# The self-attention readout of a decoder layer: sixteen 128x64 products in place of thirty-two 128x32 ones

## The chip, the cores and the metric

The kernel runs on one core of a Trainium2 chip. The metric is the device time of one execution in microseconds (us). Before the change three runs gave 231.12, 231.74 and 231.94 us, with a median of 231.74.

## The reference, cut to what matters

One pre-norm decoder layer on x of shape (32, 64, 256): self-attention with 16 heads of 16 (causal), an attention over a context of 64 rows per sequence (single head, masked), and a feed-forward block whose activations and weights are quantised.

```python
def _L0_attn_ref(x, W_qkv, W_out):
    qkv = jnp.einsum('bsd,ed->bse', x, W_qkv)
    ...
    scores = jnp.einsum('bhqd,bhkd->bhqk', Q, K) / jnp.sqrt(jnp.float32(D_K))
    scores = jnp.where(causal_mask, jnp.float32(-jnp.inf), scores)
    attn = jax.nn.softmax(scores, axis=-1)
    out = jnp.einsum('bhqk,bhkd->bhqd', attn, V)      # the readout
    ...
    return jnp.einsum('bsd,ed->bse', out, W_out)

x = x + _L0_attn_ref(_layernorm(x), W_qkv, W_out)
x = x + _L0_xattn_ref(_layernorm(x), ctx_2048, mask_BxS2_bk0)
x = x + _L0_ffn_ref(_layernorm(x), gate_w, down_w, gate_norm_w, down_norm_w)
```

## The kernel before, in words

The 2,048 rows of x are cut into T = 16 tiles of 128 rows, two sequences of 64 in each. All engines work through the same stages of every tile, each engine in an order written out by hand, and semaphores in `ev` say when a stage of tile t is done. Several tiles are under way at a time: on TensorE the attention of tile s runs beside the feed-forward of tiles s - 3 to s - 5.

TensorE's order stands in three parts. Lines 509 to 573 are a prologue, written out call by call, with the readouts of tiles 0 to 3. Then `step` (line 575) is the order of one tile's time, and a loop on TensorE's own registers (line 596) runs five turns of two steps, with the readouts of tiles 4 to 13. Lines 602 to 654 are the end, written out, with the readouts of tiles 14 and 15. In a step the order is readout, transpose_ya, cross_readout, gate_up_1, gate_up_0, transpose_yx, transpose_readout, project_qk, cross_scores, the transposes of h, project_out, scores_k, down, transpose_cross_weights, project_v, scores_q, transpose_z.

The readout multiplies the unnormalised weights `pT` by the values `v2`. ScalarE writes `pT` (line 716) from the transposed scores: on its 128 partitions lie the 64 keys of two heads of a pair, and along it the 128 queries of the tile (64 of sequence 0, then 64 of sequence 1), once for each of 8 pairs. `v2` (lines 110 and 705) is block-diagonal: for each sequence b and pair i it holds 2 x 17 columns, the 16 values and a column of ones for each head, zero on the other head's partitions. So a product has a contraction of 128, streams 34 columns of `v2`, and has some columns of `pT` as its stationary operand. It writes to PSUM bank 2, `o_ps[rows, i, :, :]`, with the queries on the partitions.

Before the change four products of 32 queries each serve one pair i (line 414): query block k goes to partitions 32k to 32k + 31, that is, to a tile of the array of 128 rows by 32 columns, and takes the values of sequence k // 2. That makes 8 x 4 = 32 products for one tile of x. All operands are float32, for which a product shows as two weight loads and two matmuls in the trace, so a readout is 64 loads and 64 matmuls there.

The readout waits for `v_d` (ScalarE has written `v2`), `exp_d0` and `exp_d1` (the halves of `pT`), and the events that free bank 2. After it come VectorE's reciprocal of the sums (line 1204) and the scaling into `oN` (line 1209), TensorE's transpose of `oN` and the output projection. `freed` (line 301) issues the waits for the former users of a bank; `within` (line 287) wraps one in a branch when its tile number is a loop variable, and returns a null context for a plain number.

Of the kernel before, what the change touches and what calls it, by code (L numbers as in the profile page):

```python
# [14 lines left out]
SEQ = 64  # L15
# [41 lines left out]
def decoder_kernel(nc, x, ctx_n, ctx_t, mask, wqkv_t, wout_t, gate_t, down_t, g_gate, g_down, const, bits, out):  # L57
    T = x.shape[0]
    with ExitStack() as stack:
        def sb(name, shape, dt=F32):  # L60
            return stack.enter_context(nc.sbuf_tensor(name, shape, dt))
# [48 lines left out]
        v2 = sb("v2", [P, 2, 2, PAIRS, 2, VW])  # L110
# [4 lines left out]
        pT = sb("pT", [P, 2, PAIRS, P])  # L115
# [34 lines left out]
        def bank(k, columns):  # L150
            return ps[:, k, 0:columns]
# [8 lines left out]
        o_ps = bank(2, PAIRS * 2 * VW).rearrange("p (i j d) -> p i j d", i=PAIRS, j=2)  # L160
# [110 lines left out]
        def _(pe):  # L271
            kept = {}

            def at(t):

                if isinstance(t, int):
                    return t
                if t.base not in kept:

                    kept[t.base] = pe.snap(t.turn * 2 + t.base if t.base >= 0 else (t.turn * 2 + t.base) & 31)  # L280
                    pe.compute_val(kept[t.base])
                return kept[t.base]
# [4 lines left out]
            def within(t, least, most):  # L287

                if isinstance(t, int):
                    return nullcontext()  # L290
                low, high = (least - t.base + 1) // 2, (most - t.base) // 2
                if low > 0 and high < TURNS - 1:
                    return pe.If((t.turn >= low) & (t.turn <= high))
                if low > 0:
                    return pe.If(t.turn >= low)
                return pe.If(t.turn <= high) if high < TURNS - 1 else nullcontext()
# [4 lines left out]
            def freed(users):  # L301

                for name, count in users:
                    with within(count, 1, T):
                        pe.wait_ge(ev[name], at(count))

            def transposes(dst, src, chunks, done, identity=ident):
# [11 lines left out]
            def transpose_ya(t, *users):  # L319
                pe.wait_ge(ev["ya_d"], at(t + 1))  # L320
                freed(users)
                transposes(xT_ps, ya[:, t % 2, :], DC, ev["yaT_ps"])

            def project_qk(t, *users):
                pe.wait_ge(ev["yaT_d"], at(t + 1))
                freed(users)
                if first(t):
                    pe.wait_ge(wqk_in, 16)
                for e in range(2 * DC):
                    for c in range(DC):  # L330
                        last = pe.matmul(qk_ps[:, e * P:(e + 1) * P], wqk[:, c, e * P:(e + 1) * P], yaT[:, t % 2, c, :],  # L331
                                         start=(c == 0), stop=(c == DC - 1))
                last.then_inc(ev["qk_ps"], 1)

            def project_v(t, *users):
                pe.wait_ge(ev["yaT_d"], at(t + 1))
                freed(users)
                if first(t):
                    pe.wait_ge(wv_in, 16)
                for b in range(2):  # L340
                    for c in range(DC):
                        for j in range(2):
                            last = pe.matmul(v_ps[SEQ * j:SEQ * (j + 1), b * P:(b + 1) * P], yaT[:, t % 2, c, b * SEQ:(b + 1) * SEQ],  # L343
                                             wv[:, c, j * P:(j + 1) * P], start=(c == 0), stop=(c == DC - 1))
                last.then_inc(ev["v_ps"], 1)
# [59 lines left out]
            def readout(t, *users):  # L405
                pe.wait_ge(ev["v_d"], at(t + 1))
                freed(users)
                for half in range(2):
                    pe.wait_ge(ev[f"exp_d{half}"], at(t + 1))
                    for g in (2 * half, 2 * half + 1):  # L410
                        for c in range(DC):
                            i = 4 * c + g
                            for k in range(4):
                                last = pe.matmul(o_ps[32 * k:32 * (k + 1), i, :, :], pT[:, t % 2, 2 * g + c, 32 * k:32 * (k + 1)],
                                                 v2[:, t % 2, k // 2, i, :, :], start=True, stop=True)
                last.then_inc(ev["o_ps_d"], 1)

            def transpose_readout(t, *users):
# [101 lines left out]
            scores_k(0, ("mx_d", 1), ("mT_d", 1))  # L520
            transpose_ya(2, ("yaT_d", 2))
            readout(0, ("q_d", 2), ("k0_d", 2), ("k1_d", 2))
            scores_q(1, ("exp_d0", 1), ("exp_d1", 1))
            project_qk(2, ("oN_d", 1))
# [3 lines left out]
            scores_k(1, ("mx_d", 2), ("mT_d", 2))  # L528
            project_out(0)
            readout(1, ("q_d", 3), ("k0_d", 3), ("k1_d", 3))  # L530
            weight_totals(("x1_d", 1))
            transpose_ya(3, ("oT_d", 1))
# [7 lines left out]
            cross_scores(0, ("yxT_d", 1))  # L540
            scores_q(3, ("exp_d0", 3), ("exp_d1", 3))
            readout(2, ("q_d", 4), ("k0_d", 4), ("k1_d", 4))
            transpose_ya(4, ("oT_d", 2))
            transpose_cross_weights(0, ("x1_d", 2))
# [1783 lines left out]
```

## Time and profile before

| what | value |
|---|---|
| median of 3 runs | 231.74 us (231.12 to 231.94) |
| the profiled execution | 231.23 us |
| its span, first to last instruction | 229.4 us |
| what lies around the span | 1.8 us |
| TensorE matmul busy | 193.2 us, 84% |
| VectorE, ScalarE, GpSimd busy | 173.6, 150.6, 135.0 us |
| mean granted TensorE clock | 0.924 of full speed |

Busy time of an engine is the union of its instructions' spans. For TensorE, PE are the matmuls and PEld the weight loads, which overlap them. In a row, `128*32 128x34` is a tile of the array of 128 rows by 32 columns and a moving operand of 128 partitions by 34 columns; `128x32` on a PEld row is the stationary operand.

### The profile page before, as it was taken

What the parts mean: (1) busy time and instruction counts of PE and PEld (TensorE: products, weight loads), DVE (VectorE), ACT (ScalarE), POOL (GpSimd) and SP (SyncE); (2) the same over time, 40 slices, a digit from 0 to 9 for tenths busy, and PEclk for the clock granted to TensorE, in tenths of its full rate; (3) what the DMA queues carried; (4) which work ended last, traced back from release to release, by engine and by line L of the source; (5) the groups of instructions that cost most, each with busy time, mean ns of one, the idle gap of its engine ahead of it and who ended that gap; (6) DMA issues with size and microseconds to landing.
All of it is one profiled execution on the core that took longest, in us unless ns stands there. A gap on an engine that the chain in (4) does not pass through costs nothing. (4 is left out here: it accounts for less than half of the span.)

```text
span 229.4 us, 11892 instructions
## 1 busy us (share of the span) xinstructions
PE 193.2 (84%) x4592; PEld 150.2 (65%) x4592; DVE 173.6 (76%) x555; ACT 150.6 (66%) x422; POOL 135.0 (59%) x290
## 2 busy tenths in 40 slices
PE   4975897898899787999999999998999887666653
PEld 4764785676678566878787868787888564434332
DVE  1234358878897777998897988988899898987750
ACT  3467446575858584788887888887868564755411
POOL 6400222456763756376776657777676698798840
PEclk9997699999999999999999999999999997957555
DMA  5998000011010200101010110102020211000011
GB/s 182 380 333 257 3 3 6 7 44 52 4 49 4 73 3 26 46 24 46 26 46 30 40 41 29 62 8 64 6 70 1 71 27 46 3 1 26 0 46 46
DMA packets 11478, 12.79 MB, mean 56 GB/s; under 512 B 1009, under 2 KB 10801, under 8 KB 11442
## 3 DMA queue, kind: packets, MB, share of 16 engines
q1 hardware_dynamic: 11442, 12.34, 16.7%
q8 instruction: 18, 0.29, 0.5%
q14 instruction: 18, 0.15, 0.2%
HBM read 10.24 MB, written 2.10 MB: 54 GB/s over the span
## 5 line engine op out<-in xcount | busy, mean ns | idle before, releaser
L331 PE MATMUL ps<-yaT,wqk 128*128 128x128 f32 x256 | 33.4, 285 | 3.2 <-issue 1.9
L2007 POOL TENSOR_TENSOR zh<-hh,gd 128x352 f32<-128x352 f32 x32 | 30.4, 955 | 7.3 <-DVE hh L1312 6.6
L331 PEld LDWEIGHTS ps<-yaT,wqk 128*128 128x128 f32 x256 | 31.5, 200 | 4.2 <-issue 2.3
L315 PE MATMUL ps<-wg,zT 128*128 128x352 bf16 x128 | 25.6, 343 | 0.9 <-ACT zT L659 0.6
L1177 DVE TENSOR_REDUCE mx<-ps 128x16 f32<-128x1024 f32 x16 | 19.5, 1220 | 7.0 <-PE ps L366 6.8
L764 ACT ACTIVATE th_sb<-ps,th 128x352 f32<-128x352 f32 x32 | 17.3, 552 | 10.0 <-PE ps L315 5.2
L1923 POOL TENSOR_TENSOR rs<-ve,neghalf 128x1 f32<-128x1 f32 x32 | 20.3, 633 | 2.7
L500 PE MATMUL ps<-wd,hT 128*128 128x256 bf16 x96 | 16.3, 317 | 5.7 <-ACT hT L659 2.8
L1921 POOL TENSOR_SCALAR ve<-mv 128x1 f32<-128x1 f32 x32 | 6.9, 215 | 23.8 <-issue 11.8
L716 ACT ACTIVATE pT<-ps 128x512 f32<-128x512 f32 x32 | 18.1, 597 | 4.0 <-PE ps L401 3.5
L659 ACT ACTIVATE hT<-ps 128x256 bf16<-128x256 bf16 (+1 forms) x32 | 15.2, 490 | 8.2 <-PE ps L309 8.1
L2029 POOL TENSOR_SCALAR hq<-zh,qh 128x704 f32<-128x704 f32 x16 | 13.6, 848 | 9.4 <-DVE qh L1341 9.1
L315 PEld LDWEIGHTS ps<-wg,zT 128*128 128x128 bf16 x128 | 13.1, 106 | 9.1 <-issue 0.9
L1299 DVE SCALAR_TENSOR_TENSOR th_sb<-th_sb,ps 128x352 f32<-128x352 f32 x32 | 16.2, 513 | 3.5 <-ACT th_sb L764 3.3
L343 PE MATMUL ps<-wv,yaT 128*64 128x128 f32 x256 | 17.7, 279 | 1.0 <-issue 1.0
L678 ACT ACTIVATE yx<-x,sh,rs 128x256 f32<-128x256 f32 x16 | 9.5, 596 | 13.0 <-POOL sh L1965 13.0
L775 ACT ACTIVATE sqj<-hh 128x352 f32<-128x352 f32 x32 | 15.9, 498 | 2.8 <-DVE hh L1312 2.6
L429 PE MATMUL ps<-wo,oT 128*128 128x256 f32 x64 | 17.5, 395 | 0.0
L1324 DVE TENSOR_REDUCE ah<-zh 128x1 f32<-128x704 f32 x16 | 14.0, 877 | 3.9 <-POOL zh L2007 2.5
L500 PEld LDWEIGHTS ps<-wd,hT 128*128 128x128 bf16 x96 | 9.4, 110 | 10.6 <-ACT hT L659 4.2
L1312 DVE TENSOR_TENSOR hh<-th_sb,ps 128x352 f32<-128x352 f32 x32 | 16.2, 513 | 0.2
L343 PEld LDWEIGHTS ps<-wv,yaT 128*64 128x64 f32 x256 | 13.7, 136 | 3.7 <-issue 3.4
(121 smaller groups left out, 517.5 us busy)
## 6 DMA issues: line engine op xcount, KB each, us to landing
ct_in<-ctx_t SPq DMA_DIRECT2D x16, 128.0 KB, 2.1
cn_in<-ctx_n SPq DMA_DIRECT2D x16, 128.0 KB, 2.2
out<-o_out SPq DMA_DIRECT2D x16, 128.0 KB, 1.7
wg<-gate_t SPq DMA_DIRECT2D x1, 1408.0 KB, 8.2
x_in<-x SPq DMA_DIRECT2D x1, 1024.0 KB, 9.8
wd<-down_t SPq DMA_DIRECT2D x1, 640.0 KB, 8.2
wqk<-wqkv_t SPq DMA_DIRECT2D x1, 512.0 KB, 3.9
x_in<-x SPq DMA_DIRECT2D x1, 512.0 KB, 8.5
```

Source lines behind the costliest of these rows:

```text
L315: last = pe.matmul(bank[:, :], zT[:, t % 2, c, :], wg[:, c, first:first + HALF], start=(c == 0), stop=(c == DC - 1))
L331: last = pe.matmul(qk_ps[:, e * P:(e + 1) * P], wqk[:, c, e * P:(e + 1) * P], yaT[:, t % 2, c, :], start=(c == 0), stop=(c == DC - 1))
L343: last = pe.matmul(v_ps[SEQ * j:SEQ * (j + 1), b * P:(b + 1) * P], yaT[:, t % 2, c, b * SEQ:(b + 1) * SEQ], wv[:, c, j * P:(j + 1) * P], s ...
L429: last = pe.matmul(y_ps[:, :], oT[:, t % 2, c, :], wo[:, c, :], start=(c == 0), stop=(c == DC - 1))
L500: last = pe.matmul(d_ps[:, :], hT[:, t % 2, c, :], wd[:, c, :], start=(c == 0), stop=(c == IC - 1))
L716: nc.scalar.activation(pT[:, t % 2, 4 * half:4 * half + 4, :].rearrange("p (g c) t -> p g (c t)", g=2), psS[:, 2 * half:2 * half + 2, 256: ...
L764: nc.scalar.activation(th_sb[:, t % 2, j, :], g_ps[j], ACT.Tanh, scale=col(th, t)).then_inc(ev[f"tanh_d{j}"], 1)
L1177: V.tensor_reduce(out=mx[:, t % 2, :, :], in_=scores, op=ALU.max, axis=AX).then_inc(ev["mx_d"], 1)
L1299: V.scalar_tensor_tensor(out=th_sb[:, t % 2, j, :], in0=th_sb[:, t % 2, j, :], scalar=1.0, in1=g_ps[j], op0=ALU.add, op1=ALU.mult).then_in ...
L1312: V.tensor_tensor(hh[:, t % 2, j * HALF:(j + 1) * HALF], th_sb[:, t % 2, j, :], u_ps[j], ALU.mult).then_inc(ev[f"hh_d{j}"], 1)
L1923: G.tensor_tensor(col(rs, t), col(ve, t), neghalf[:, :], ALU.pow).then_inc(ev[f"rstd{n}"], 1)
L2007: G.tensor_tensor(zh[:, t % 2, part], hh[:, t % 2, part], gd[:, part], ALU.mult).then_inc(ev[f"zh_d{j}"], 1)
```

## The change

Each pair's four products of 32 queries become two of 64 queries, one for each sequence b. Each takes `pT`'s 64 columns of that sequence and the same 34 columns of `v2`, and writes to partitions 64b to 64b + 63, a tile of the array of 128 rows by 64 columns. A readout has 16 products instead of 32. The waits, the order of calls and the operands are the same. The other hunk moves the test for a plain number from `within` to its caller.

```diff
             def freed(users):
                 for name, count in users:
-                    with within(count, 1, T):
+                    with within(count, 1, T) if not isinstance(count, int) else nullcontext():
                         pe.wait_ge(ev[name], at(count))
...
                         for c in range(DC):
                             i = 4 * c + g
-                            for k in range(4):
-                                last = pe.matmul(o_ps[32 * k:32 * (k + 1), i, :, :], pT[:, t % 2, 2 * g + c, 32 * k:32 * (k + 1)],
-                                                 v2[:, t % 2, k // 2, i, :, :], start=True, stop=True)
+                            for b in range(2):
+                                last = pe.matmul(o_ps[SEQ * b:SEQ * (b + 1), i, :, :], pT[:, t % 2, 2 * g + c, SEQ * b:SEQ * (b + 1)],
+                                                 v2[:, t % 2, b, i, :, :], start=True, stop=True)
                 last.then_inc(ev["o_ps_d"], 1)
```

## Rows read from the trace of the kernel before

**Rows 1.** The page: span, busy time, and granted clock in 40 slices.

```profile
span 229.4 us, 11892 instructions
PE 193.2 (84%) x4592; PEld 150.2 (65%) x4592; DVE 173.6 (76%) x555; ACT 150.6 (66%) x422; POOL 135.0 (59%) x290
PEclk9997699999999999999999999999999997957555
```

**Rows 2.** Busy time by stretch: prologue, turns 1, 2 and 5 of the loop, end.

```profile
0.00:63.70 63.70, 50.49 (x1328) 41.98 (x1328) 36.72 (x118) 37.63 (x94) 24.40 (x60) 0.95 0.35 114
63.70:89.85 26.15, 22.36 (x584) 17.54 (x572) 20.30 (x71) 16.52 (x50) 15.56 (x36) 1.00 0.11 34
89.85:112.20 22.35, 21.65 (x574) 17.64 (x572) 20.10 (x61) 18.82 (x56) 14.51 (x32) 1.00 0.11 33
...
156.60:178.50 21.90, 21.37 (x572) 17.55 (x572) 19.91 (x68) 17.97 (x54) 14.44 (x30) 1.00 0.12 37
178.50:229.40 50.90, 34.03 (x406) 20.40 (x405) 37.13 (x114) 24.58 (x70) 35.08 (x70) 0.72 0.10 30
```

**Rows 3.** Waits of PE, 90 to 180 us.

```profile
PE ps L414 <- issue: 1.5, 3, 0.6
PE ps L414 <- ACT v L659: 0.4, 1, 0.4
PE ps L309 <- ACT zT L659: 0.3, 1, 0.3
```

**Rows 4.** PE and PEld in order of time, 101 to 102 us: one readout.

```profile
101.06 0.77 PE L414 MATMUL ps<-v,pT 128*32 128x34 f32 x64
```

```profile
101.06 0.66 PEld L414 LDWEIGHTS ps<-v,pT 128*32 128x32 f32 x64
```

**Rows 5.** Groups by form, whole span: loads and matmuls of float32 in three tile widths.

```profile
L414 PE MATMUL ps<-v,pT 128*32 128x34 f32 x1024 | 12.7, 199 | 3.6 <-issue 2.4 <-ACT pT L716 0.7 <-ACT v L659 0.4
```

```profile
L331 PEld LDWEIGHTS ps<-yaT,wqk 128*128 128x128 f32 x256 | 31.5, 200 | 4.2 <-issue 2.3 <-ACT yaT L659 1.8
L414 PEld LDWEIGHTS ps<-v,pT 128*32 128x32 f32 x1024 | 10.9, 109 | 6.5 <-issue 5.4 <-ACT v L659 0.5
L447 PEld LDWEIGHTS ps<-ct_in,yxT 128*64 128x64 f32 x128 | 5.3, 138 | 1.2 <-issue 1.2
```

**Rows 6.** Project_v's first loads, counted in 20 ns windows (PE, then PEld).

```profile
121.38:121.40 0.02, 0.01 (x2) 0.02 (x2) 1.00 0.00 0
121.40:121.42 0.02, 0.02 (x2) 0.02 (x2) 1.00 0.00 0
121.42:121.44 0.02, 0.02 (x2) 0.02 (x3) 1.00 0.00 0
121.44:121.46 0.02, 0.02 (x2) 0.02 (x4) 1.00 0.00 0
```

**Rows 7.** In order of time: cross_scores and project_v, both on 128x64 tiles.

```profile
117.66 0.43 PE L447 MATMUL ps<-ct_in,yxT 128*64 128x64 f32 x8
...
121.39 1.09 PE L343 MATMUL ps<-wv,yaT 128*64 128x128 f32 x16
```

```profile
117.63 0.31 PEld L447 LDWEIGHTS ps<-ct_in,yxT 128*64 128x64 f32 x8
```

**Rows 8.** Waits of PE, 0 to 91 us, and of PE, 190 us to the end.

```profile
PE ps L500 <- issue: 2.1, 1, 2.1
PE ps L331 <- issue: 1.9, 1, 1.9
...
PE ps L395 <- issue: 0.3, 1, 0.3
```

```profile
PE ps L500 <- ACT hT L659: 2.8, 3, 1.3
```

**Rows 9.** DMA queues: the instruction queue in 0:91, and in 84.75:87.06.

```profile
q8 instruction: 15, 0.25, 1.1%
```

```profile
q8 instruction: 1, 0.02, 2.5%
```

## The prediction

> **What bounds the kernel now.** I read the page first, then busy time by stretch, then TensorE's waits, and last the readout in order of time. The page [rows 1] gives TensorE 193.2 us of 229.4, an average over unlike stages. By stretch [rows 2] a later turn of TensorE's loop (two tiles of x) takes 21.9 to 22.4 us and its matmuls are busy for 97% of it (21.65 of 22.35), while VectorE has 20.10. The waits of 90 to 180 us [rows 3] come to 2.2 us on TensorE, nearly all before a readout. So from tile 4 on TensorE's own stream sets the pace, and what a readout takes longer or shorter moves everything behind it. The prologue (63.7 us, 50.5 busy), the first turn (26.15 us against 22) and the end (50.9 us, 34 busy, clock down to 0.72) have idle time, where a change can be partly hidden.
>
> **The readout now.** One takes 0.77 us from its first matmul's start to its last one's end, its loads 0.66 us [rows 4]. One matmul's record is 199 ns [rows 5], nearly all of it latency, so 64 records start within 0.57 us: 9 ns each, 36 ns on each of the four column tiles. Sixteen readouts make the 12.7 us of the group.
>
> **What a record costs on its tile.** It has to load its stationary columns and stream its 34. The stream: project_v streams 128 columns on two 128x64 tiles, 16 records in 1.09 us [rows 7]; less one record of 0.28 us, 15 starts in 0.81, 54 ns each or 108 ns per tile, 0.85 ns a column. So 34 columns stream in 29 ns, whatever the tile's width. The load: the float32 loads last 109, 138 and 200 ns for 32, 64 and 128 columns [rows 5], 0.9 to 1.0 ns for each further column. So 32 columns load in 27 to 31 ns and 64 in 54 to 62. A second reading goes by starts: project_v's first two loads start at 121.38 to 121.39, one for each tile, and the next two follow by 121.44 [rows 6], 50 to 60 ns later, while tiles of the same line work side by side. A third: cross_scores loads 64 columns eight times, four on each tile, within 0.31 us [rows 7]; less one record of 0.138, three steps of 57 ns. Its stream is 64 columns (54 ns), so this row bounds the load's step from above.
>
> **The change part by part.** Half the products go: of 64 loads and 64 matmuls a readout keeps 32 of each. But the array work of a tile does not shrink. Before, four tiles had 16 records each; now two tiles have 16 each. Per tile the stream stays at 16 x 29 = 0.46 us. Only the load grows, from 27 to 31 ns, which hid behind the 29 of the stream, to 55 or so, which no longer does. So the step on a tile becomes that of the load:
> - new readout, first load to last matmul's start: 0.055 + 15 x 0.057 = 0.91 us;
> - old readout, the same: 0.57 to 0.59 us, by the rows above;
> - difference: +0.33 us a readout.
>
> What the halved instruction count buys on the array is the difference between 36 ns per tile and the 29 to 31 that load and stream need, and it is spent as soon as the load is the bound. Bounds of this term: below, the load hidden wholly, 16 x 30 = 0.48 us, -0.09; above, load and stream of a tile one after the other, 16 x (55 + 29) = 1.34 us, +0.77. I take the middle value since the cross_scores row has the very tile, type and load.
>
> **How many count.** Tiles 4 to 13 in the loop and 14 and 15 behind it feed a saturated stream or the chain that leads to the end (there TensorE waits for ScalarE's copies of `hT` [rows 8], which wait for earlier work of the same tile): 12 x 0.33 = 4.0 us. The readouts of tiles 0 to 3 lie where TensorE idles 13 us anyway; I count half, +0.6. VectorE has 2 us of room in a turn, so no other engine takes over; the reciprocal and `oN` just come later, with gate_up between them and the transpose that wants them.
>
> **Instruction loading.** The waits before 91 us [rows 8] show stretches with nothing to wait for but "issue": seven rows from 2.1 to 0.3 us, 9.3 us in all. In the 2.1 us one a packet of the instruction queue moves, one of 15 in the first 91 us [rows 9]. I read this as TensorE waiting for code that it meets for the first time. In the prologue and the first turn it runs 1,912 matmuls and 1,900 loads [rows 2]; over 15 packets that is an estimate of some 254 records a packet. A readout sheds 64 records; four in the prologue and two in the loop body are 384, one and a half packets. At 9.3 / 15 = 0.6 us a packet that is -0.9 us. The packets' borders also move, each to a place where a full queue hides it or where none does. A single one is worth 0 to 2.1 us; over the 14 left I give this plus or minus 2 us. The hunk in `freed` is worth nothing: for a plain number `within` returned a null context before.
>
> **The sum.** +4.0 + 0.6 - 0.9 = +3.7 us. The profiled execution took 231.23 us, 0.5 under the median of 231.74; 231.23 + 3.7 = 234.9, and from the median 235.4. I forecast 235.4 us.
>
> **A rule weighed.** The rows show starts 9 ns apart across the column tiles and, within a tile, loads that run during the stream: project_v has 108 ns per tile and record, where load and stream in turn would make 55 + 108. The Trainium skill, "TensorE: Matmul & The Clock Gate", Part 3, says that a weight load overlaps matmuls in flight only when the row group differs; here all tiles use all rows. By that rule the new readout would be at the upper bound, 1.34 us, and the sum +10 us. The trace speaks against it, but it speaks against this change, so it is a rival below. The same page ("Wait — 56ns, not 53.3ns?") states that start-to-start never drops below about 25 ns; by that halving the count would save 32 x 25 ns a readout. The 9 ns of this trace contradict it.
>
> **The rivals.**
> - *The load hides after all* (faster). If the load of 64 columns took no longer than the stream, a tile's step would be 30 ns and each readout 0.09 us shorter: 16 x -0.09 = -1.4, with -0.9 of code 229.4 us. It decides at a load under about 36 ns. For it: fewer instructions to issue. Against it: three readings of 54 to 62 ns. 6%.
> - *Code borders pay for it* (no change). The array loses its 4.0 us, but two packets fewer and luckier borders before 91 us give 3 or more back: 231.5 to 232.9. For it: 9.3 us of "issue" to win from. Against it: it needs a third of them. 9%.
> - *Load and stream in turn* (much slower). +0.77 for each of 14 readouts, less 0.9: 241.6 us. 3%.
> - *A wait takes it up*. TensorE's 0.4 to 0.6 us before the readout at each turn's head could shrink as the readout grows. It comes before the readout, and what ends it ("issue", and `v2` after TensorE's own project_v) is itself late when TensorE is late. Were it absorbed, a turn would lose 0.2 instead of 0.66 us: about 233. 5%, part of the range.
> - *A dearer prologue*. All 16 readouts count and the borders fall badly: 238. 10%, part of the range.
>
> **How the numbers follow.** A measurement of this kernel can tell about 0.5%, 1.2 us, from no change, so slower begins at 232.9. Forecast with its two near variants 82%, of which a little ends under 232.9 by lucky borders. Slower 0.85, same 0.08, faster 0.07. The range leaves out the faster rival, most of the lucky borders and the far slower one: 232.6 to 238.2.
>
> **What the next profile would show.** The group of line 414 with 512 matmuls, `128*64 128x34`, in one readout 32 records over about 1.08 us (0.77 now), and some 17 us in the whole; PEld records of 138 ns in place of 109; a later turn of 22.6 to 23.0 us; 1 to 2 instruction packets fewer. I am wrong if a readout stays at or under 0.77 us (the load was hidden), if it is near 1.5 us (in turn), if a turn grows by much less than two readouts do (slack in the loop), or if the time before 90 us moves by more than 2 us (code loading).

## The result, and the profile after

The changed kernel takes 227.73 us (median of 22 runs, 224.91 to 230.54) against 231.43 us for the kernel before (22 runs, 227.28 to 236.20). The ratio, which is taken over the undisturbed runs of both and is therefore nearer to 1 than the medians are, is 0.9897, with a 95% interval of 0.9857 to 0.9937: 2.4 us faster, where I forecast 3.7 us slower.

Not all of a run's time lies in the span from its first to its last instruction. In 61 executions of the kernel before 1.8 to 1.9 us lay outside it; with the changed kernel it was 1.8 us in two of 22, the profiled one among them, and 2.5 to 3.1 us in the other twenty. So the span became some 3.2 us shorter, and 0.8 us came back outside it. No run shows what these 0.8 us are. Two variants below have them in every execution (wide_loop_only, wide_padded), and two never have them (wide_prologue_only, wide_shift_back).

The page of the changed kernel, the lines that answer to [rows 1] and [rows 9]:

```profile
span 224.3 us, 10868 instructions
PE 194.4 (87%) x4080; PEld 153.6 (68%) x4080; DVE 173.4 (77%) x555; ACT 150.3 (67%) x422; POOL 135.6 (60%) x290
PEclk9999999999999999999999999999999998876955
...
q8 instruction: 16, 0.26, 0.5%
```

TensorE has 512 matmuls and 512 loads fewer, and is busy for longer, 194.4 us instead of 193.2. The 0.7 and 0.6 in the clock's row between 17 and 29 us [rows 1] are gone.

One readout in the loop, PE and PEld in order of time, and the group of line 414 in the whole span, answering to [rows 4, 5]:

```profile
95.49 1.13 PE L414 MATMUL ps<-v,pT 128*64 128x34 f32 x32
```

```profile
95.49 1.01 PEld L414 LDWEIGHTS ps<-v,pT 128*64 128x64 f32 x32
```

```profile
L414 PE MATMUL ps<-v,pT 128*64 128x34 f32 x512 | 18.4, 225 | 3.1 <-issue 2.1
L414 PEld LDWEIGHTS ps<-v,pT 128*64 128x64 f32 x512 | 16.7, 137 | 6.0 <-issue 5.0
```

The readout itself is slower by just what was forecast: from first start to last end 1.13 us (0.77), from first load to last matmul's start 0.90 to 0.93 us (0.57 to 0.59; forecast 0.91). Thirty-two records at 137 ns a load make (1.01 - 0.137) / 15 steps = 58 ns on each of the two tiles; I had said 57.

Busy time by stretch, in the order PE, PEld, DVE, ACT, POOL, clock, answering to [rows 2]: up to the readout of tile 4, then turns 1, 2 and 5 of the loop, then the rest.

```profile
0.00:59.20 59.20, 49.39 (x1201) 41.25 (x1201) 36.98 (x119) 37.47 (x95) 25.09 (x61) 1.00 0.38 123
59.20:84.40 25.20, 23.02 (x509) 18.21 (x509) 20.52 (x70) 16.89 (x50) 15.74 (x35) 1.00 0.11 34
84.40:107.10 22.70, 22.34 (x508) 18.32 (x508) 20.11 (x62) 18.39 (x55) 14.48 (x32) 1.00 0.11 36
...
152.70:175.50 22.80, 22.72 (x510) 18.66 (x510) 20.29 (x69) 18.15 (x53) 14.61 (x31) 1.00 0.13 41
175.50:224.30 48.80, 32.43 (x339) 20.58 (x338) 35.99 (x112) 24.20 (x69) 34.74 (x69) 0.77 0.09 28
```

So the two profiled executions, 229.4 and 224.3 us of span, differ by stage like this (starts of the readouts of tiles 4, 6 and 14, read from the order of time):

| stage | before, us | after, us | difference |
|---|---|---|---|
| start to readout of tile 4 | 64.0 | 59.2 | -4.8 |
| turn 1 of the loop | 26.3 | 25.2 | -1.1 |
| turns 2 to 5 | 89.0 | 91.2 | +2.1 |
| readout of tile 14 to the end | 50.1 | 48.7 | -1.3 |

The saturated turns lose 0.53 us each on average (0.37 to 0.68). Everything that was gained came earlier, in the stretch where code is met for the first time, and some at the end. TensorE's waits of the first 91 us, answering to [rows 8], the first lines behind the opening wait for the constants:

```profile
PE ps L401 <- issue: 2.2, 1, 2.2
PE ps L309 <- DVE zb L1295: 1.2, 2, 0.9
PE ps L414 <- issue: 1.1, 3, 0.7
```

Of seven "issue" rows with 9.3 us two are left with 3.3. The 2.1 us before line 500 and the 1.9 us before line 331 are gone. The question for the runs was why: because sixteen products are better than thirty-two there, or because the code has moved against the borders of the blocks in which it is loaded.

### The profile page after: what moved, and what is told of

It reads as the page before. It is cut to its first block and busy times, and to the rows that moved or that the text cites. A ratio compares the mean times of both kernels' runs of the same rounds, so it can differ in the third digit from the quotient of the medians.

```text
span 224.3 us, 10868 instructions
## 1 busy us (share of the span) xinstructions
PE 194.4 (87%) x4080; PEld 153.6 (68%) x4080; DVE 173.4 (77%) x555; ACT 150.3 (67%) x422; POOL 135.6 (60%) x290
## 5 line engine op out<-in xcount | busy, mean ns | idle before, releaser
L331 PE MATMUL ps<-yaT,wqk 128*128 128x128 f32 x256 | 31.5, 276 | 0.9 <-ACT yaT L659 0.7
L331 PEld LDWEIGHTS ps<-yaT,wqk 128*128 128x128 f32 x256 | 29.9, 192 | 1.7 <-ACT yaT L659 1.4
L315 PE MATMUL ps<-wg,zT 128*128 128x352 bf16 x128 | 24.3, 330 | 0.6 <-ACT zT L659 0.6
L414 PE MATMUL ps<-v,pT 128*64 128x34 f32 x512 | 18.4, 225 | 3.1 <-issue 2.1
L414 PEld LDWEIGHTS ps<-v,pT 128*64 128x64 f32 x512 | 16.7, 137 | 6.0 <-issue 5.0
L500 PE MATMUL ps<-wd,hT 128*128 128x256 bf16 x96 | 15.7, 308 | 3.8 <-ACT hT L659 2.8
L315 PEld LDWEIGHTS ps<-wg,zT 128*128 128x128 bf16 x128 | 12.5, 102 | 8.3 <-ACT zT L659 1.0
```

The lines of the kernel that those rows point to most:

```text
L315: last = pe.matmul(bank[:, :], zT[:, t % 2, c, :], wg[:, c, first:first + HALF], start=(c == 0), stop=(c == DC - 1))
L414: last = pe.matmul(o_ps[SEQ * b:SEQ * (b + 1), i, :, :], pT[:, t % 2, 2 * g + c, SEQ * b:SEQ * (b + 1)], v2[:, t % 2, b, i, :, :], start=T ...
```

## The experiments

Two theories. **A**: a wide readout costs some 0.33 us of array time wherever it stands; the gain is where the borders of the instruction blocks fall. **B**: the halved count of products is what helps. Later A was split into A1 (the places of the borders) and A2 (the pace: fewer instructions handed out during more array time, so that the queue is fuller at a border).

### Each half of the change alone

The tile's width is made a variable; it is 64 for some readouts and 32 for the others.

```diff
+                            width = SEQ if isinstance(t, int) and t < 4 else 32    # wide_prologue_only
+                            width = 32 if isinstance(t, int) and t < 4 else SEQ    # wide_loop_only
+                            for k in range(P // width):
+                                part = slice(width * k, width * (k + 1))
+                                last = pe.matmul(o_ps[part, i, :, :], pT[:, t % 2, 2 * g + c, part],
+                                                 v2[:, t % 2, width * k // SEQ, i, :, :], start=True, stop=True)
```

> 128x64 tiles for the readouts of tiles 0 to 3 alone, 128x32 from tile 4 on. Theory A (the wide readout costs 0.33 us on the array each time, and the gain of the change is where the borders of the instruction blocks fall before 90 us): the readout of tile 4 starts near 59 us as in the changed kernel (64.0 before), a later turn of the loop is back at 22.3 us (22.8 in the changed one), the whole about 1% under the changed kernel, ratio 0.975 to 0.985. Rival B (the halved count of products is what helps, in the loop as well): the loop gains nothing from going back, ratio 0.99 or above.

> 128x32 tiles for the readouts of tiles 0 to 3, 128x64 from tile 4 on. Theory A: the prologue is that of before (readout of tile 4 near 64 us, with a stall of about 2 us in the project_qk of tile 2), a later turn takes 22.8 us, ratio 1.005 to 1.015. Rival B: some gain is left, ratio under 1.0.

Measured against the kernel before: wide in the prologue alone 0.9899 (0.9771 to 1.0027), wide from tile 4 on 1.016 (1.0048 to 1.0272), each from four runs. The first lies above the 0.975 to 0.985 that I had expected, with an interval that holds both theories; the second is 0.001 above its range. By stretch, first wide_prologue_only, then wide_loop_only (up to tile 4, turns 1 and 5):

```profile
0.00:61.80 61.80, 52.85 (x1200) 44.30 (x1201) 37.01 (x119) 37.52 (x95) 23.98 (x61) 0.94 0.35 118
61.80:88.10 26.30, 22.36 (x572) 17.56 (x573) 20.43 (x70) 16.51 (x49) 15.79 (x35) 1.00 0.11 33
154.90:177.10 22.20, 22.12 (x574) 17.86 (x574) 20.20 (x69) 17.88 (x53) 14.53 (x31) 1.00 0.13 41
```

```profile
0.00:63.60 63.60, 50.18 (x1328) 41.50 (x1328) 36.79 (x119) 37.90 (x95) 24.32 (x60) 0.97 0.35 115
63.60:88.70 25.10, 23.22 (x508) 18.32 (x508) 20.42 (x70) 16.82 (x50) 15.69 (x35) 1.00 0.11 35
157.00:179.90 22.90, 22.82 (x512) 18.70 (x512) 20.39 (x69) 18.18 (x53) 14.70 (x31) 1.00 0.13 40
```

The later turn follows the width of the loop's readout and nothing else: 22.2 us narrow, 22.9 wide. In all fourteen profiles of this study turns 2 to 5 average 22.22 to 22.28 us with the narrow readout and 22.78 to 22.79 with the wide one. B has fallen for the loop. With the narrow prologue the readout of tile 4 is back at 63.7 us, and the wide loop alone makes the kernel slower. The loss that I forecast for the loop is there, and the gain sits ahead of it. My 59 us for the prologue-only kernel was missed by 2.8 us; the section on the clock below says where they lie.

### The narrow kernel with its code moved

```diff
+            pe.addr_align(256, offset=0, max_nops=0)      # narrow_shift_on: offset=128
             pe.wait_ge(cst_in, 16)
             for _ in range(WARM):
```

> The kernel before with its code moved against the borders of the instruction blocks: TensorE's code is aligned so that its first wait stands at slot 0 of a block of 256 (it stands at about slot 65 now), so all borders come 65 instructions later; nothing else changes. Theory A: the readout of tile 4 starts at another time by 1 us or more either way, and the stalls called issue stand before other lines; later turns stay at 22.3 us. Rival B: everything stays within 1 us.

> The kernel before with its first wait at slot 128 of a block of 256, so all borders come 63 instructions earlier. That moves the border after the one in scores_k of tile 0 out of project_qk of tile 2. Theory A: the 1.9 us stall before line 331 goes or moves, and the start of the readout of tile 4 moves by 1 us or more. Rival B: everything stays within 1 us.

Measured: shifted back 1.0041 (0.9988 to 1.0094), shifted on 1.0025 (0.9972 to 1.0078). The whole hardly moves, but the stalls do. The readout of tile 4 starts at 66.6 us in the kernel shifted back (64.0 before) and at 64.0 in the one shifted on: there the stall before line 331 is gone, as expected, but others took its place, and the start did not move by the 1 us that I had expected. The readout of tile 0 in the kernel shifted back, in order of time, and then the "issue" rows of TensorE's waits, 3 to 91 us, in the kernel shifted on:

```profile
19.33 0.39 PE L414 MATMUL ps<-v,pT 128*32 128x34 f32 x20 [0.43 <-ACT pT L717]
23.59 0.89 PE L414 MATMUL ps<-v,pT 128*32 128x34 f32 x44 [3.87 <-issue]
```

```profile
PE ps L414 <- issue: 2.4, 4, 1.0
PE ps L395 <- issue: 2.3, 1, 2.3
PE ps L366 <- issue: 1.8, 1, 1.8
...
PE ps L343 <- issue: 0.8, 1, 0.8
```

A readout is torn in two for 3.87 us, with nothing to wait for. Counting TensorE's instructions in the trace from its first weight load (loads, matmuls and its sequencer's semaphore waits, in order of their starts), these are the numbers of the ones that start 0.35 us or more after the one before them and share one remainder modulo 256, up to 91 us (nearly all gaps at other numbers stand before instructions that wait for a semaphore):

```
kernel                   instruction behind the gap            number mod 256   sum of gaps, us
before                   447 703 1471 1727 1983 2239 3775      191              10.6
wide_loop_only           447 703 1471 1727 1983 2239           191               8.1
after                    447 959                               191               2.8
wide_prologue_only       447 3519                              191               4.5
narrow_shift_back        512 1024 1536 2048 2304                 0               8.3
narrow_shift_on          384 640 1664 3200 3456                128               7.7
```

The stalls stand 256 instructions apart, and move by exactly the 65 and 63 slots by which the code was moved. They also follow the instruction queue: in the kernel before, its packets begin at 21.3 and 84.8 us, and numbers 703 and 3775 start at 23.7 and 87.1. Each of the seven starts 2.2 to 2.7 us after the last packet. That ties them to the loading of code, and it gives the block's size. The Trainium skill, "Runtime: NRT & Kernel Launch", section "Instruction fetch mechanics", gives the same 256 instructions to a block and an instruction memory for TensorE that holds eight; that agrees with the loop: a turn has some 1,200 of TensorE's instructions, fewer than five blocks, and from 91 to 180 us the instruction queue of [rows 9] moves no packet in the kernel before. It also says that crossing a block's border is mostly hidden; here seven of the 16 crossings of the first 91 us come with a gap, and a gap is up to 3.9 us of idle time.

My reading is that a border costs something when TensorE has too little in hand when it comes to it. In the kernel before, number 703 is the third matmul of project_qk of tile 2, close behind a wait for `oN`: 2.3 us. One readout earlier has shed 64 instructions in the changed kernel, so its border 703 lies in project_v of tile 2, behind the 16 long matmuls of project_qk, and no gap is seen.

### The wide kernel with its code moved, and with the old places restored

wide_padded puts unused slots, jumped over, behind each prologue readout, so that all code behind it has the slots that it has in the kernel before. Its products are those of the changed kernel.

```diff
             readout(0, ("q_d", 2), ("k0_d", 2), ("k1_d", 2))
+            pe.addr_align(256, offset=152, max_nops=0)
...
             readout(1, ("q_d", 3), ("k0_d", 3), ("k1_d", 3))
+            pe.addr_align(256, offset=144, max_nops=0)
...
             readout(2, ("q_d", 4), ("k0_d", 4), ("k1_d", 4))
+            pe.addr_align(256, offset=238, max_nops=0)
...
             readout(3, ("q_d", 5), ("k0_d", 5), ("k1_d", 5))
+            pe.addr_align(256, offset=60, max_nops=0)
```

> The changed kernel, with unused instruction slots (jumped over, not run) behind each readout of the prologue, so that all code from there on has the slots that it has in the kernel before: as many blocks to load, borders at the same instructions. Theory A1 (the saved blocks and the new places of the borders give the gain): the stalls at the borders of before return (project_qk of tile 2, cross_scores of tile 0, project_v of tile 3), the readout of tile 4 starts at 63.5 to 66 us (59.2 without the padding), ratio to before 1.00 to 1.015. Theory A2 (the gain is pace: a wide readout hands out half as many instructions while the array works longer, so the queue is fuller when a border comes): the stalls stay short wherever the borders lie, readout of tile 4 at 59 to 61.5 us.

> The changed kernel with its first wait at slot 0 of an instruction block (borders 65 instructions later). A1 (the changed kernel's borders lie luckily): readout of tile 4 later by 1 us or more than 59.2, stalls at the borders add up to 5 us or more (2.8 in the changed kernel, 10.6 in the one before), ratio to before near 1.0. A2 (pace): within 1 us of the changed kernel, stalls at borders under 5 us.

> The changed kernel with its first wait at slot 128 (borders 63 instructions earlier). A1: stalls at the borders add up to 5 us or more, readout of tile 4 later by 1 us or more than 59.2. A2: within 1 us of the changed kernel.

> 128x64 tiles for the readouts of tiles 0 to 3 alone, with the first wait at slot 128. Its loop has the narrow readout, so a later turn takes 22.3 us. A1: its prologue differs from that of the unshifted one (readout of tile 4 at 61.8 us with 6.8 us of half clock) by 1 us or more. A2: within 1 us at the same clock. In both cases 0.5 us a turn faster than the kernel that is wide throughout with the same shift.

Measured: wide_padded 1.0088 (1.0034 to 1.0141), wide_shift_back 1.0025 (0.9977 to 1.0073), wide_prologue_shift_on 0.9939 (0.9884 to 0.9995). wide_shift_on had a median of 231.88 us of four runs beside 231.16, too few for a ratio. TensorE's waits of the first 91 us in the padded kernel, the rows put to "issue", and then the torn readout of tile 0 in wide_shift_back:

```profile
PE ps L401 <- issue: 2.2, 1, 2.2
PE ps L447 <- issue: 1.1, 1, 1.1
...
PE ps L331 <- issue: 0.8, 1, 0.8
PE ps L343 <- issue: 0.7, 1, 0.7
```

```profile
19.64 0.78 PE L414 MATMUL ps<-v,pT 128*64 128x34 f32 x20 [0.43 <-ACT pT L717]
23.43 0.54 PE L414 MATMUL ps<-v,pT 128*64 128x34 f32 x12 [3.02 <-issue]
```

With the old slots the old stalls are back, before lines 331, 447 and 343, one of 2.2 us before line 401 has come, at a border where the kernel before has none, and the readout of tile 4 starts at 66.8 us, even later than I had put it. Of that, 1.4 us is not the padding's: the profiled execution (234.58 us, over the median of 233.77) starts the readout of tile 0 at 20.9 us, ahead of all moved code, where the changed kernel does at 19.4. The jumps over the unused slots are not what costs: behind the readouts of tiles 0 and 2 the next matmul follows the last one of the readout after 0.15 us in both kernels, and all four jumps together delay it by under 0.4 us. The same array work at other slots goes from 0.9897 to 1.0088 of the kernel before: 1.9%, 4.4 us, each measured beside runs of the kernel before; wide_shift_back, whose only addition stands ahead of TensorE's first wait, is 1.3% above the changed kernel. That is the size of the layout's effect, with what it does to the clock in it.

The padded kernel doesn't separate the places of the borders from the number of blocks. Its 15th packet comes at 91.9 us, at the end of its first turn of the loop, so it loads as many blocks up to there as the kernel before (15), and the changed kernel loads 14 in its first 91 us. In the window 0 to 92 us:

```profile
q8 instruction: 15, 0.25, 1.1%
```

wide_shift_back separates them. In 0 to 91 us it loads 14, as the changed kernel does, and yet its readout of tile 4 starts at 63.6 us instead of 59.2:

```profile
q8 instruction: 14, 0.23, 1.1%
```

So one block less is not what gave the gain; the borders' places matter at the same count of blocks. A1 was too strong in another point: it wanted 5 us of gaps or more in both shifted kernels, and there are 3.2 us in wide_shift_back and 3.9 in wide_shift_on (6.3 in wide_padded), as A2 had it. But A2 wanted the time to stay within 1 us, and the readout of tile 4 starts at 63.6 and 65.9 us. In wide_prologue_shift_on it starts at 66.0 us (61.8 unshifted), as A1 had it, and turns 2 to 5 take 22.24 us on average, 0.55 less than in wide_shift_on. The time does not follow the sum of the gaps. The interval from the readout of tile 0 to that of tile 1 shows it best:

```
kernel                 us from readout 0 to readout 1   gap at a border     us at half clock in it
after                   7.7                             none                none
wide_prologue_only     10.1                             none                5.9
wide_padded            11.1                             1.1, 2.4 (640, 896) none
before                 11.6                             2.3 (number 703)    6.8
wide_shift_back        12.3                             3.2 (number 512)    3.4
narrow_shift_back      13.1                             4.1 (number 512)    6.8
```

In the changed kernel the one long gap, 2.4 us in scores_k of tile 0, ends before this interval; the readout of tile 0 starts at 19.4 us all the same, as it does in kernels that have no gap there (19.6 in wide_shift_back). A gap costs what it costs only where no other wait covers it.

B falls for the prologue too as the whole cause: wide_padded and wide_shift_back have the products of the changed kernel, one for one, without its gain. With the borders of before, four wide readouts are no help at all: from the readout of tile 0 to that of tile 4 wide_padded takes 45.9 us and wide_loop_only, with narrow ones in the prologue, 44.7, both with 3.4 us at half clock. Whether the smaller count helps on the average over layouts stays open. With the narrow loop, three layouts of a narrow prologue gave 1 (the kernel before), 1.0025 and 1.0041, and the four of a wide one, with the runs of the next section, 0.9767 to 0.9899, 0.9788, 0.9939 and, by medians alone, 0.993: all lower. Seven layouts are few, and the runs don't tell luck from fewer blocks or a fuller queue in this.

### The version with both, measured again

> The changed kernel itself once more, on the chip of the next three, as their measure: 0.985 to 0.994 of the kernel before.

> 128x64 tiles for the readouts of tiles 0 to 3 alone, measured again with more rounds. The loop's five turns give back 0.5 us each and the two readouts behind it 0.3 each, about 3.3 us, less the stall of some 2 us that its other borders cause in the first turn: about 1 us under the changed kernel, ratio to before 0.982 to 0.99. If the narrow loop is worth nothing in the whole, it equals the changed kernel.

> The same with the first wait at slot 96 of an instruction block (borders 31 instructions earlier). If borders are what counts, the stalls of the first 90 us stand before other lines and the time moves by up to 2 us either way; later turns at 22.3 us.

> The same with the first wait at slot 32 (borders 33 instructions later). The first border after the start then falls into or near the readout of tile 0, as in the two kernels shifted back, which lost 3 to 4 us there: slower than the unshifted one by 1 us or more.

The edits are those above; the directive of the last two says offset=96 and offset=32:

| kernel | median, us (runs) | ratio to before | 95% interval |
|---|---|---|---|
| changed_again | 228.37 (12) | 0.9911 | 0.9862 to 0.9959 |
| wide_prologue_again | 225.60 (6) | 0.9767 | 0.9714 to 0.9821 |
| wide_prologue_slot_96 | 226.17 (7) | 0.9788 | 0.9735 to 0.9842 |
| wide_prologue_slot_32 | 228.96 (6) | none given | |

The change is confirmed. Wide in the prologue and narrow in the loop beats both kernels: 2.3% under the one before, and 1.5% under the changed one, 0.9767 / 0.9911 = 0.985. I had expected 1 us there, and it is 3.3 (0.0144 of 231 us), give or take up to 1.7 by the two intervals. The loop gives back 2.1 us, the two readouts behind it nothing that shows, and about 0.9 us is the time outside the span: 1.8 us in all six runs of wide_prologue_again, 2.7 on average in those of the changed kernel. The 1.8 us gap that this layout has in turn 1 (number 3519 again) seems to cost little. Slot 96 is as good within the intervals. Slot 32 has the expected gap of 1.8 us inside the readout of tile 0 and a median 3 us higher, but its six runs reach from 225.17 to 230.23 us, too wide to call it dearer.

## Why the prediction was wrong

**The bound.** Right. TensorE's stream sets the pace of the loop, and a readout's extra time mostly passes into the turn: behind the readouts of tiles 8, 9 and 10 every later call of the step starts 0.370, 0.358 and 0.368 us later than before, counted from the readout's start. Not behind all of them. The kernel before waited for `zT` behind the readout of tile 7 (the 0.3 us of [rows 3]), and the wider readout filled this wait; first before, then after:

```profile
101.06 0.77 PE L414 MATMUL ps<-v,pT 128*32 128x34 f32 x64
102.08 0.41 PE L309 MATMUL ps<-cst,ya 128*128 128x128 f32 x2 [0.26 <-ACT zT L659]
```

```profile
95.49 1.13 PE L414 MATMUL ps<-v,pT 128*64 128x34 f32 x32
96.55 0.44 PE L309 MATMUL ps<-cst,ya 128*128 128x128 f32 x2
```

There the later calls start only 0.06 us later, and by shorter waits of this kind 0.17 and 0.28 us behind the readouts of tiles 11 and 13. The wait at the turn's head gave back 0.02 to 0.05 us. So of the 0.73 us that two readouts could cost, turn 3 lost 0.68, and turns 2 to 5 lost 0.53 on average, for which I had said 0.66. The rival "a wait takes it up" came true for some 0.2 us a turn, at another wait than the one that it named.

**The cost of a wide product.** Right: 58 ns a step on a tile (57), 0.90 to 0.93 us a readout (0.91), 0.36 us more where no wait gives way (0.33). That fits the load of 64 float32 columns as the bound, as its three readings said. Neither the rival in which the load hides nor the one in which load and stream take turns came true; by the latter a step would be 84 ns.

**How many count.** Wrong in part. Eight of the ten readouts in the loop count, in turns 2 to 5; turn 1 takes 25.0 to 25.2 us with wide readouts and 24.9 to 25.1 with narrow ones where no gap of some 2 us lies in it (narrow_shift_back, slots 32 and 96). The 0.66 us behind the loop is not to be seen: the end takes 48.7 us in the changed kernel, 48.6 with narrow readouts (wide_prologue_only) and 48.4 with wide ones (wide_loop_only). The 50.1 us of the profile before were an execution with a lower clock there, 0.72 against 0.77. Over the fourteen profiles the end goes with TensorE's time at half clock in it and not with the readout's width: 47.3 us with 16.0 at half clock, 48.7 with 22.2 (the changed kernel), 50.1 with 28.1 (the kernel before).

**Instruction loading.** This is the step that failed. I had seen the stalls, put them to code, and found the size of a block (254 records by my estimate; it is 256). Then I gave the term an average, 0.6 us a packet times one and a half packets, -0.9 us, with 2 us either way for the moved borders. The runs show in its place that moved borders, with what they do to the clock, are worth 1.3% to 1.9% (3 to 4.4 us) between layouts of the same wide kernel. Between the two profiled executions, the 5.1 us of span are 2.1 us lost in turns 2 to 5, some 2 to 2.5 us of clock in the prologue and 1.3 us of clock in the end gained (see below), and the rest, about 3.5 us, gained in the prologue and turn 1 where the borders moved, net of what six wide readouts cost there. That is four times the term's -0.9 us and beyond its bound of -2.9. The clock was no term of my sum at all. The average over all runs is less, 3.2 us of span, and 0.8 us outside it; how these split between borders and clock no run shows exactly. The rival "code borders pay for it" was the nearest one; it had the borders give back the loss and no more, and I gave it 9%.

**What the profile could have said.** The numbers of the stalled instructions stand in the trace of the kernel before: 447, 703, 1471 and so on, 256 apart. With that, the new place of each border follows from the order of calls, and I could have seen that the costly one in project_qk of tile 2 moves behind 16 long matmuls. What each border then costs would still have been a guess: [rows 8] shows gaps from 0.3 to 2.1 us, and other crossings none. I took a mean over borders where a list was to be had.

**The clock.** In the profile before TensorE ran at half its clock for 6.8 us of the prologue (a mean of 0.62 over 9 us). Granted clock and TensorE's busy time from 19 to 28 us, in the kernel before, the changed kernel, and wide_prologue_only:

```profile
19.00:28.00 9.00, 6.87 (x144) 0.62 0.30 96
```

```profile
19.00:28.00 9.00, 8.16 (x239) 1.00 0.27 84
```

```profile
19.00:28.00 9.00, 8.81 (x173) 0.63 0.30 94
```

The last two run the same code up to 59 us. Without the fall to 1.2 GHz the readout of tile 4 starts at 59.2 and 59.7 us (after, changed_again), with it at 61.8 and 62.2 (wide_prologue_only and again). Those are 2.5 us, of which 0.3 to 0.8 lay ahead of the readout of tile 0 already, so the fall costs some 2 us or a little more. So of the 4.8 us between the profiles of before and after, about half is the clock of two executions. Before the fall TensorE had idled for 1.6 us (before) and 2.0 us (wide_prologue_only) at the gap in scores_k of tile 0, and again for 0.4 and 0.2 us before the readout; the changed kernel had idled for 2.2 and 0.4 us there and kept its clock. It isn't only the luck of two profiles: the mean granted clock is 0.946 in the 34 of the changed kernel and 0.935 in the 61 of the one before, some 24 and 30 us at half clock. Whether shorter stalls make the fall rarer stays open; no run separates it.

## What to carry to other kernels

Code that is met for the first time is loaded in blocks, and a border was free or cost microseconds in these runs, it seems by what was queued in front of it. An edit that changes the number of instructions in unrolled code moves every later border, so its gain there may be luck of the layout: check it by shifting the code of both versions, and judge the edit itself by a stretch that loads nothing, such as a later turn of a loop. Compare the time at half clock as well, and the time outside the span. A narrower tile of the array is the better one where the weight load is the bound: here 128x64 float32 tiles with 34 streamed columns took 58 ns a step for two tiles, 128x32 ones some 36 ns for four.

## What the runs showed of the hardware that I had not expected

The instruction that follows an uncovered block border started 0.4 to 4.1 us after the one before it, in every shifted kernel at a number modulo 256 that moves with the code, slot by slot. A block border can lie inside a readout and tear it in two. A readout that grew by 0.36 us moved later calls of the saturated loop by 0.36 to 0.37 us where nothing waited, and by as little as 0.06 us where a short wait stood behind it.
